# Folding a residual into a weight matrix: the identity added once to the routed layer's chosen matrix

## What is computed

```python
# sublayer 0: gated recurrence over time, 16 heads of 8
x = _layernorm(x + _L0_attn_ref(x, ...))
# sublayer 1: one expert of 8 for all tokens
idx = jnp.argmax(jax.nn.log_softmax(logits) + gumbel)
out = jnp.einsum('btd,de->bte', x, W[idx]) + b[idx]
x = _layernorm(x + out)
# sublayer 2: linear attention, dots @ proj, no softmax, then mixer_w, mixer_b
x = _layernorm(x + _L1_attn_ref(x, ...))
# sublayer 3: silu(x w1) * (x w2), two gelu layers of 512, then w3
x = _layernorm(x + _L1_ffn_ref(x, ...))
```

## Time and profile before

| | us |
|---|---|
| median of 3 runs | 228.05 |
| lowest and highest | 226.93, 228.31 |
| the profiled execution | 228.93 |
| its span | 227.1 |

### The profile page before, as it was taken

One profiled execution on the slowest core, in us unless ns is written; L12 is line 12 of the kernel. 1 busy time (PEld: TensorE's weight loads), 2 busy tenths in 40 slices (PEclk: granted clock), 3 DMA queues, 4 the chain that ended last, 5 costly groups with the idle time before them and its releaser, 6 DMA issues.

```text
span 227.1 us, 3170 instructions
## 1 busy us (share of the span) xinstructions
PE 195.5 (86%) x972; PEld 145.8 (64%) x972; DVE 160.6 (71%) x385; ACT 112.7 (50%) x172; POOL 92.7 (41%) x70
## 2 busy tenths in 40 slices
PE   7576886978798799999999999999997989989950
PEld 6135672536576568778977878798675767756830
DVE  0379957899996688989769799777896206673043
ACT  2487204262415676131289643224996155896630
POOL 4026004938201650672435829424369324165401
PEclk9967999699999999999999999999999699999995
DMA  5993020100000010000000010000001000001001
GB/s 144 344 425 152 0 72 1 46 0 0 0 3 0 0 51 1 0 3 0 3 0 0 9 38 0 0 0 0 0 0 51 0 0 3 0 0 49 0 0 46
DMA packets 6125, 8.19 MB, mean 36 GB/s; under 512 B 480, under 2 KB 4832, under 8 KB 5728
## 3 DMA queue, kind: packets, MB, share of 16 engines
q1 hardware_dynamic: 6112, 8.02, 10.3%
HBM read 6.97 MB, written 1.05 MB: 35 GB/s over the span
## 4 chain that ended last, share of the span: by engine, by line
issue 31%; PE 23%; POOL 20%; DVE 12%; ACT 5%; DMA 4%; SPq 2%; POOLq 1%; DVEq 0%
PE c_bank L811 11%; POOL rstd L286 5%; POOL hid_even_low L309 5%; DMA mlp_pack<-mlp 4%; POOL hid_odd_low L309 4%; PE y_bank L780 3%; POOL res L281 3%; DVE read L581 3%; DVE state L573 2%; DVE normed_lent L558 2%; PE b_bank L799 2%; PE b_bank L950 2%; POOL mlp_low L305 2%; ACT hidden_pack L422 1%; PE b_bank L794 1%
## 5 line engine op out<-in xcount | busy, mean ns | idle before, releaser
L286 POOL TENSOR_TENSOR rstd<-varied,power 128x4 f32<-128x4 f32 x16 | 17.8, 1114 | 66.9 <-DVE varied L551 66.9
L780 PEld LDWEIGHTS y_bank<-attend_pack,read 128*128 128x128 f32 x256 | 32.3, 196 | 17.8 <-DVE read L581 16.5
L780 PE MATMUL y_bank<-attend_pack,read 128*128 128x128 f32 x256 | 36.0, 287 | 8.7 <-DVE read L581 8.2
L573 DVE TENSOR_TENSOR_SCAN state<-rep_bank,keep 128x256 f32<-128x256 f32 x64 | 39.8, 669 | 2.8 <-PE rep_bank L772 2.6
L309 POOL TENSOR_TENSOR hid_even_low<-hidden_pack,hid_even_high 128x512 fp32r<-128x512 f32 x16 | 20.3, 1282 | 36.0 <-ACT hidden_pack L422 26.4
L581 DVE TENSOR_TENSOR read<-state,query 128x512 f32<-128x512 f32 x32 | 25.2, 796 | 0.0
L420 ACT ACTIVATE hid_even_high<-c_bank,scales_pack 128x512 fp32r<-128x512 f32 x16 | 11.0, 688 | 27.7 <-PE c_bank L811 27.7
L422 ACT ACTIVATE hidden_pack<-c_bank,scales_pack 128x512 f32<-128x512 f32 x32 | 21.8, 682 | 0.0
L811 PE MATMUL c_bank<-hid_even_high,hidden_high 128*128 128x512 f32 x64 | 19.7, 414 | 0.6 <-ACT hidden_pack L397 0.5
L811 PE MATMUL c_bank<-hid_odd_low,hidden_high 128*128 128x512 f32 x64 | 19.5, 414 | 0.7 <-DVE hid_odd_low L593 0.4
L811 PE MATMUL c_bank<-hid_odd_high,hidden_high 128*128 128x512 f32 x64 | 19.9, 424 | 0.0
(11 more groups left out here) (129 smaller groups left out, 375.8 us busy)
## 6 DMA issues: line engine op xcount, KB each, us to landing
hidden_pack<-hidden SPq DMA_DIRECT2D x2, 1024.0 KB, 12.1
attend_pack<-attend SPq DMA_DIRECT2D x1, 1152.0 KB, 8.0
xT_lent<-x_chan SPq DMA_DIRECT2D x4, 256.0 KB, 8.8
xt<-x_tok SPq DMA_DIRECT2D x4, 256.0 KB, 3.0
mlp_pack<-mlp SPq DMA_DIRECT2D x1, 768.0 KB, 10.2
out<-xT_lent SPq DMA_DIRECT2D x3, 256.0 KB, 2.3
metric_pack<-metric SPq DMA_DIRECT2D x1, 384.0 KB, 13.6
project_pack<-project SPq DMA_DIRECT2D x1, 256.5 KB, 2.7
```

Of the source, the lines that this page charges most:

```text
L286: nc.gpsimd.tensor_tensor(rstd[n][:], varied[n][:], power[:], ALU.pow).then_inc(ln_rstd[n], 1)
L573: ins = nc.vector.tensor_tensor_scan(state[:, e % STATES, at], rep_bank[e % 2][:, at], keep[:, bass.ds(a * T + s * SEQ, SEQ)], 0.0, ALU.ad ...
L780: ins = nc.tensor.matmul(y1_bank[:, tile(j)], read[:, e % READS, tile(j)], out_w_rep_sb[:, e, :], start=(e == 0 and j == 0), stop=False, s ...
```

## The change

GpSimd no longer makes res1. In place of the wait for `ln_out[0]` and the four `residual(1, a)`, it makes once, in `step(0, None, None)`, a new tensor `passed_w` = chosen matrix + identity (128x128), after waits for the chosen matrix and the metric pack. TensorE multiplies x1T by `passed_w` instead of `chosen_w`, so the product holds the residual, and waits for `passed_ready` in its first use. VectorE's `norm_sum(1)` adds the chosen bias, repeated over the four tiles, to the bank, and no longer waits for GpSimd's res1. The tensor res1 is gone.

```diff
@@ GpSimd, step
                     inverse_std(0, a)
-                    pool.wait_ge(ln_out[0], nth(a, NT, NT))
                     if first(a):
                         pool.wait_ge(chosen_loaded, 32)
-                    residual(1, a, res1, normed[0], chosen_b)
+                        pool.wait_ge(loaded["metric"], 16)
+                        nc.gpsimd.tensor_tensor(passed_w[:], chosen_w[:], ident_sb, ALU.add).then_inc(passed_ready, 1)
@@ VectorE, norm_sum
                 dve.wait_ge(ready, value_)
-                dve.wait_ge(res_ready[n], nth(group, 1, 1))
-                nc.vector.tensor_tensor(total[n][:], bank_[:], (res0, res1, res2, res3)[n][:],
-                                        ALU.add).then_inc(summed, 1)
+                if n == 1:
+                    if first(group):
+                        dve.wait_ge(chosen_loaded, 32)
+                    view = "p (j c) -> p j c"
+                    nc.vector.tensor_tensor(total[1].rearrange(view, j=NT), bank_[:].rearrange(view, j=NT),
+                                            chosen_b[:].unsqueeze(1).to_broadcast([P, NT, P]),
+                                            ALU.add).then_inc(summed, 1)
+                else:
+                    dve.wait_ge(res_ready[n], nth(group, 1, 1))
+                    nc.vector.tensor_tensor(total[n][:], bank_[:], (res0, None, res2, res3)[n][:],
+                                            ALU.add).then_inc(summed, 1)
@@ TensorE, step
                     if first(b):
-                        pe.wait_ge(chosen_loaded, 32)
+                        pe.wait_ge(passed_ready, 1)
...
-                    per_tile(b5_bank, x1T, lambda j: chosen_w[:]).then_inc(b_ready, 1)
+                    per_tile(b5_bank, x1T, lambda j: passed_w[:]).then_inc(b_ready, 1)
```

More of the change, by code:

```diff
@@ L125, in build @@
         chosen_w, chosen_b = sb("chosen_w", [P, P]), sb("chosen_b", [P, P])
+        passed_w = sb("passed_w", [P, P])
         proj_metric = sb("proj_metric", [P, P])
@@ L151, in build @@
         x3T_parts = [sb(f"x3T_{which}", [P, T], F32R) for which in ("high", "low")]
-        res1, res2, res3 = sb("res1", [P, T]), sb("res2", [P, T]), sb("res3", [P, T])
+        res2, res3 = sb("res2", [P, T]), sb("res3", [P, T])
         heads, moved = xT_lent[0], xT_lent[1]
@@ L177, in build @@
             sem("pm_copied"))
+        passed_ready = sem("passed_ready")
         proj_ready, proj_out = sem("proj_ready"), sem("proj_out")
```

## The result

| | median us | lowest to highest | runs | profiled execution | its span |
|---|---|---|---|---|---|
| before | 228.18 | 226.93 to 230.44 | 4 | 228.93 | 227.1 |
| changed | 236.08 | 235.31 to 237.25 | 4 | 237.25 | 235.5 |

The ratio is 1.037, 95% interval 1.0298 to 1.0441: slower by 7.9 us by the medians and 8.4 us by the ratio, where 6.4 was forecast. In a second comparison, beside the experiments, the same kernel had a ratio of 1.0182 (1.0084 to 1.0281) to the kernel before, 4.2 us. The forecast lies between the two.

The account below looks back on a forecast made before the run. The bound was a chain of waits through VectorE and TensorE, which GpSimd instructions block by whole-instruction turns. Terms 5.26 + 0.8 - 0.6 + 0.9 = +6.4 us on 228.05 gave 234.4 us, range 231.0 to 236.2.

Parts of the forecast that it names:

- The product at half clock: TensorE's product after the first norm_out starts at 1.2 GHz and takes at most 2.10 us, not 1.20: +0.8 us.
- the read's -0.6: VectorE's read at 45.77 us no longer meets the weight cut and shortens from 1.28 to 0.67: -0.6 us.
- stretch A: From first to second GpSimd rstd, norm 0 to norm 1 of group 0: forecast +5.26 + 0.8 - 0.6 = 5.46 us.
- The second place: At 76 us, GpSimd's low_part(0, 0) now runs amid norm_out(0, 1) and delays its last tiles: +0.9 us.
- All before 37.8 stays as it is: Everything in the kernel before 37.8 us, ahead of the first norm_out's transposes, was to stay unchanged.
- constant from there: The delay was to be 5 to 6 us at 55 us, 6 to 7 at 90 us, then unchanging.
- stretch C: From thirteenth to fourteenth GpSimd rstd, where the change touches nothing; no difference was forecast.
- stretch B: From fourth GpSimd rstd (norm 0 of group 1) to the fifth: forecast at +0.9 us.
- only moving the wait away matters: Of four res1 removals, two were worth 0; in the other two, only moving GpSimd's ln_out[0] wait counted.
- The last tile did not escape: Rival: VectorE gets two turns between two of GpSimd's, so norm_out's last tile passes the cut: +3.2, 231.3 us, chance 0.10.
- Not slower: Rival: GpSimd starts its three instructions only after norm_out, so nothing is blocked: 226.9 us, chance 0.14.
- Larger: Rival: the add costs 1.27 us (+0.8) and TensorE's clock returns late (+0.4): 235.6 us, chance 0.06.

Follow-up runs that it names:

- the spacer: Changed kernel with GpSimd's wait for ln_out[0] in all steps and, in the first step, an unread addition of res1's size: 228.5 us against 228.12, ratio 1.0028.
- the cut held back: Changed kernel with GpSimd's wait for ln_out[0] in all steps and cut_weights(1) waiting for VectorE's dvalue steps: 227.83 us against 229.0, ratio 0.9925.

## Why the prediction was right and where it missed

**The bound and the mechanism: right.** A whole GpSimd instruction against one VectorE tile, turn by turn: `norm_out` was to take 43.68 - 37.30 = 6.38 us and took 6.40. The add was put at 0.45 and took 0.45. The undisturbed cut shows 4.50 for 4.41. The exclusive lock that the Trainium skill ("SBUF — State Buffer", section "Who interferes with whom") describes agrees with these lines: a tile of 0.34 us lasted 4.51 beside the whole cut.

**The mechanism as I stated it is too wide.** I wrote that a VectorE instruction with all operands in SBUF and a GpSimd tensor_tensor exclude each other. `norm_stats` has all its operands in SBUF and isn't held where the two meet. In the kernel before its four instructions lie wholly inside a GpSimd low part that has its undisturbed 1.27 us. GpSimd's and VectorE's timelines:

```profile
151.62 1.27 POOL L309 TENSOR_TENSOR hid_even_low<-hidden_pack,hid_even_high 128x512 fp32r<-128x512 f32 x1 [5.04 <-ACT hidden_pack L422]
151.89 0.87 DVE L541 BATCH_NORM_STATS2 stats<-normed_lent 128x6 f32<-128x128 f32 x4
```

No term of the sum used such an instruction. The ones seen held are tensor_scalar, cast and two-input tensor_tensor from SBUF.

**The product at half clock: right,** 2.05 us for 1.97 to 2.10; with the read's -0.6 and the hidden dvalue steps, stretch A makes +5.61 for a forecast of 5.46.

**The second place: right by itself, short by its clock.** `norm_out(0, 1)` takes 2.06 us instead of 1.11; this is the timeline of VectorE, with GpSimd's low part between:

```profile
83.81 2.06 DVE L569 TENSOR_SCALAR normed<-total,moments,rstd 128x128 f32<-128x128 f32 x4
```

```profile
83.97 1.30 POOL L312 TENSOR_TENSOR hid_even_low<-hidden_pack,hid_even_high 128x512 fp32r<-128x512 f32 x1 [0.32 <-ACT hid_even_high L405]
```

But after TensorE's longer wait there the clock fell as well, which the term of +0.9 left out: it was priced only at the first place. The term measured +1.91 in this profile, and +0.90 to +1.59 in the four others that lack the wait at this place. TensorE's busy time in the changed kernel:

```profile
85.00:86.00 1.00, 0.59 (x3) 1.00 0.00 0
...
88.00:89.00 1.00, 1.00 (x4) 0.50 0.00 0
...
91.00:92.00 1.00, 1.00 (x5) 1.00 0.02 7
```

**The steps that failed: the second place at +0.9, "All before 37.8 stays as it is", and a shift "constant from there".** The first is the term above, short by 1.0 us. Besides it, two stretches that the change doesn't touch, and that I put at nothing, vary between executions. One is the start: the first rstd comes at 36.1 to 38.6 us in the profiles with whole cuts (one at 35.6). Part of it is what `cut_weights(0)` catches. In the kernel before it caught a small routing step, in the changed one the first read, on which TensorE waits. VectorE's timeline of the kernel before:

```profile
15.83 0.67 DVE L581 TENSOR_TENSOR read<-state,query 128x512 f32<-128x512 f32 x1
...
17.60 3.28 DVE L506 TENSOR_SCALAR route<-route 128x8 f32<-128x8 f32 x1
```

and of the changed one:

```profile
16.61 3.91 DVE L592 TENSOR_TENSOR read<-state,query 128x512 f32<-128x512 f32 x1
```

That explains only a part: in the second profile of the changed kernel the cut caught a routing step again (2.65 us), and the first rstd still came at 37.78. The two profiles differ by 0.85 us, which is about what the catch can be worth of the 2.39. In both profiles of the changed kernel the first scan also starts 0.8 to 1.1 us later than in the kernel before (14.26, 14.59 and 13.49), and the clock is at half from 19 to 25 us, where it is mostly full in the kernel before. What makes the start differ stays open. With the cuts in pieces this mark is at 34.3 to 34.7 in all three profiles. The other is stretch C, 17.1 us in seven profiles and 18.5 to 18.7 in six, with the same waits in it. Busy time of TensorE in the kernel before:

```profile
174.00:176.00 2.00, 0.62 (x2) 1.00 0.00 0
176.00:178.00 2.00, 1.59 (x6) 0.76 0.00 0
178.00:180.00 2.00, 2.00 (x6) 0.50 0.00 0
```

and in the changed kernel, shifted by 9.91 us:

```profile
183.91:185.91 2.00, 0.60 (x2) 1.00 0.00 0
185.91:187.91 2.00, 1.61 (x8) 1.00 0.00 0
187.91:189.91 2.00, 2.00 (x13) 1.00 0.00 0
```

The engine's idle share is the same, and the clock falls in one and not in the other. Why is open. It is not the time in the span at which the stretch begins, by itself: in two profiles it began at 176.80 and 176.85 us and took 17.11 and 18.69. In the span of the changed profile these gave +2.39 and -1.55 and the clock of stretch B +1.0: together 1.8 us above the 6.5 that the change makes by itself. How they fell in the unprofiled runs isn't seen. Two comparisons of +8.4 and +4.2 us around the 6.5 fit such a spread, but that the first lies outside the range because of it is argued, not shown.

**A wrong sentence that the sum did not need.** I wrote that "only moving the wait away matters". With the wait back, A lost 2.86 of its 5.61 us, and 1.03 us were added behind A; the rest came back only with the spacer or with the cut held back. The removed addition itself stood between VectorE's dvalue_low and a 4.4 us instruction. Had the change kept the wait, I would have forecast no loss and been wrong by 3.8 us.

**The rivals.** The last tile did not escape: 6.40 us. "Not slower" needed GpSimd to start after `norm_out`; it started 0.07 us ahead. "Larger" named a late clock, and it was late: TensorE's clock came back only between 52 and 53 us, and the replicates ran at half clock as they did before. Of the 0.4 us priced for that at most 0.15 shows in stretch A, and the add cost 0.45 us and not 1.27.

## What to carry to other kernels

Taking work off an engine with slack moves everything queued behind it forward: before a removal, read what comes next in that queue and what it will meet, since an instruction of 1.3 us was worth 3.6 us as a spacer here. A long GpSimd tensor_tensor held VectorE's tensor_scalar, cast and two-input tensor_tensor instructions with their operands in SBUF until its end, whatever their size (a 128x8 step lasted 3.28 us); `norm_stats` ran beside a GpSimd low part without being held. Pieces of 512 columns kept each hold under 1.3 us and brought 2 to 3.3 us here; the fold by itself is not shown to bring anything. Where a wait of an engine looks needless, look at what its neighbour does in that time.

## What the runs showed of the hardware

- GpSimd and VectorE, each with instructions of the kinds named above queued, took turns instruction by instruction in the stretches shown: add, tile, residual, tile, cut, tile, tile made 6.40, 6.40, 6.42 and 6.42 us in the four profiles without the wait.
- Not every VectorE instruction on SBUF takes part: four of `norm_stats`, 0.87 us together, ran inside a GpSimd instruction of 1.27 us, and neither was stretched.
- The granted clock in one and the same stretch fell or did not fall from profile to profile, worth 1.57 us (C: 17.11 or 18.68), and 18 small products in a gap of 6.4 us kept it up in one profile and not in the next (A: 16.55 and 17.93).
- A bias read four times over from one 128x128 tile costs VectorE nothing beside a dense tile: 684 against 687 ns.
